# Attention with eight matmuls of values per unit or sixteen, and the entering batch's steps one to two units later

## The reference

```
h  = relu(layernorm(x))
z  = layernorm((L_norm @ h) @ Wc + bc) * g1 + be1
x1 = relu(z) + h
q, k, v = x1 @ Wq, x1 @ Wk, x1 @ Wv          # 4 heads
scores  = where(adjacency > 0, q k^T / sqrt(32), -1e9)
o  = softmax(scores) @ v                       # per head
x2 = layernorm(x1 + o @ Wo + bo) * g2 + be2
out = x + layernorm(x2 + gelu(x2 @ W1 + b1) @ W2 + b2) * g3 + be3
```

## Time and profile before

| | |
|---|---|
| median of 3 runs | 1015.18 us (1006.49 to 1015.77) |
| the profiled execution | 1019.77 us, its span 1017.9 us |
| mean granted clock of TensorE | 0.955 of 2.4 GHz |
| PE busy, share of the span | 937.3 us, 92% |
| DVE, ACT, POOL busy | 617.8, 535.1, 318.9 us (61%, 53%, 31%) |
| DMA moved | 61.54 MB; k and q take the greater part |

### The profile page before, as it was taken

One profiled execution on the slowest core, in us unless ns is written; L12 is line 12 of the kernel. 1 busy time (PEld: TensorE's weight loads), 2 busy tenths in 40 slices (PEclk: granted clock), 3 DMA queues, 4 the chain that ended last, 5 costly groups with the idle time before them and its releaser, 6 DMA issues. The chain is left out here.

```text
span 1017.9 us, 20046 instructions
## 1 busy us (share of the span) xinstructions
PE 937.3 (92%) x7078; PEld 757.7 (74%) x7078; DVE 617.8 (61%) x2003; ACT 535.1 (53%) x1176; POOL 318.9 (31%) x421
## 2 busy tenths in 40 slices
PE   5998999999999999989699999999999999876995
PEld 4556789999999999978466777777777777655774
DVE  3752333333333333524578988888888888864886
ACT  2232322222222233121588888888888888862674
POOL 0001101111111111203135544555555544222786
PEclk8887999999999999989799999999999999995998
DMA  3000000000000000003354444454545554500122
GB/s 91 1 1 10 11 1 12 20 10 10 10 10 10 10 10 10 12 1 102 87 131 116 118 114 116 114 121 110 124 125 125 126 125 126 126 2 1 42 62 63
DMA packets 47218, 61.54 MB, mean 60 GB/s; under 512 B 4377, under 2 KB 22050, under 8 KB 47138
## 3 DMA queue, kind: packets, MB, share of 16 engines
q1 hardware_dynamic: 47138, 60.51, 23.1%
HBM read 39.53 MB, written 20.97 MB: 59 GB/s over the span
## 5 line engine op out<-in xcount | busy, mean ns | idle before, releaser
L1562 ACT ACTIVATE prob<-prob,low 128x512 f32<-128x512 f32 x256 | 184.0, 719 | 51.4 <-DVE low L1614 49.5
L1614 DVE CUSTOM_DVE_ANT_0 prob<-bank,mask 128x512 f32<-128x512 f32 x256 | 171.5, 684 | 28.6 <-PE bank L1440 27.0
L1453 PE MATMUL bank<-ident,prob 128*128 128x128 f32 x1024 | 161.9, 281 | 12.0 <-ACT probT L1551 11.8
L1453 PEld LDWEIGHTS bank<-ident,prob 128*128 128x128 f32 x1024 | 113.8, 141 | 58.1 <-issue 31.7
L1440 PE MATMUL bank<-k_stack,q_stack 128*128 128x512 f32 x256 | 123.8, 485 | 10.2 <-DVE low L1614 5.0
L1551 ACT ACTIVATE probT<-bank 128x512 f32<-128x512 f32 x176 | 102.6, 583 | 2.9 <-PE bank L1453 1.1
L1083 DVE TENSOR_TENSOR T_lo<-bank,T_hi 128x512 fp32r<-128x512 f32 x48 | 33.1, 689 | 111.9 <-ACT T_hi L921 111.9
L921 ACT ACTIVATE T_hi<-bank 128x512 fp32r<-128x512 f32 x48 | 28.4, 592 | 134.7 <-PE bank L831 91.7
L619 POOL TENSOR_SCALAR var_eps<-mv 128x4 f32<-128x4 f32 x16 | 3.6, 226 | 297.7 <-DVE mv L1036 297.7
L927 ACT ACTIVATE Sq<-bank,trace_inv 128x512 fp32r<-128x512 f32 x64 | 44.0, 687 | 92.3 <-PE bank L754 92.3
L1473 PE MATMUL bank<-probT,v 128*32 128x128 f32 x2048 | 82.3, 279 | 3.2 <-ACT probT L1551 1.1
(11 more groups left out here) (241 smaller groups left out, 1948.1 us busy)
## 6 DMA issues: line engine op xcount, KB each, us to landing
k_stack<-bounce_q SPq DMA_DIRECT2D x64, 256.0 KB, 5.2
q_stack<-bounce_k SPq DMA_DIRECT2D x64, 256.0 KB, 7.6
bounce_q<-k_parts SPq DMA_DIRECT2D x16, 512.0 KB, 2.8
bounce_k<-q_parts SPq DMA_DIRECT2D x16, 512.0 KB, 3.1
x_in<-in_x_dram SPq DMA_DIRECT2D x16, 256.0 KB, 2.7
out_dram<-result SPq DMA_DIRECT2D x16, 256.0 KB, 2.2
A<-in_adj_dram SPq DMA_DIRECT2D x4, 256.0 KB, 3.3
W1s<-in_L_gnn_W_dram SPq DMA_DIRECT2D x1, 128.0 KB, 2.3
```

Of the source, the lines that this page charges most:

```text
L1453: last = pe.transpose(psum[2 + u % 2][:, mt * P:(mt + 1) * P], prob[u % RING][:, mt * P:(mt + 1) * P], ident[:, :])
L1562: act.activation(prob[u % RING][:, :], prob[u % RING][:, :], ACT.Exp, bias=low[:, u % TURNED:u % TURNED + 1], scale=-1.0, accum_out=row_su ...
L1614: dve.tensor_tensor_reduce(prob[u % RING][:, :], psum[u % 2][:, :], mask[:, u // HEADS, :], 1.0, 3e38, ALU.add, ALU.min, low[:, u % TURNED ...
```

## The change

The constants of the entering batch's steps and of the spread are raised by one or two units, and VALUES_STEP goes from 2 to 4. Nothing else is changed: the same instructions run, in another order on PE, ACT and DVE. By engine and unit:

- x1's transposes and x1T out from unit 2 to 3; the product with Wk and k_hi from 3 to 5; that with Wq and q_hi from 4 to 6; k_lo from 4 to 6, q_lo from 5 to 7
- the spread transposes from PE unit 3 to 4, their copy from ACT unit 4 to 5
- all four blocks of a tile's values in one unit: tile 0 in 7, tile 1 in 11, tile 2 in 15, tile 3 in unit 3 of the next round

SP's program is unchanged, and so is the unit of score 0, residual, v, oT, the convolution and the projection.

```
-AT_X1, AT_X1T, AT_X1T_OUT, AT_K, AT_Q, AT_K_HI, AT_Q_HI, AT_K_LO, AT_Q_LO = 1, 2, 2, 3, 4, 3, 4, 4, 5
+AT_X1, AT_X1T, AT_X1T_OUT, AT_K, AT_Q, AT_K_HI, AT_Q_HI, AT_K_LO, AT_Q_LO = 1, 3, 3, 5, 6, 5, 6, 6, 7
 AT_V, AT_V_OUT = 14, 14
 AT_CONV, AT_CONV_OUT, AT_Z, AT_Z_OUT, AT_Z_MOMENTS, AT_Z_STD = 6, 9, 10, 11, 12, 14
 AT_Y_MOMENTS, AT_H = 9, (11, 12, 13, 15)
-AT_RINV, AT_SPREAD, AT_SPREAD_OUT, AT_O, AT_PROJ, AT_Z2 = 0, 3, 4, 8, 11, 12
+AT_RINV, AT_SPREAD, AT_SPREAD_OUT, AT_O, AT_PROJ, AT_Z2 = 0, 4, 5, 8, 11, 12
 AT_Z2_MOMENTS, AT_Z2_STD = 3, 5
 TURN_LAG = 3
 VALUES_LAG = 7
-VALUES_STEP = 2
+VALUES_STEP = 4
```

## The result

The changed kernel takes 1055.2 us in the median of 4 runs (1048.2 to 1059.2); its ratio to the kernel before is 1.040 (95% interval 1.032 to 1.049), so 40 us slower where 26 were forecast. Put on the 1015.2 us of the kernel before, the ratio gives 1056.2, just over the upper end of the range, 1056. The profiled execution has a span of 1057.4 us, 39.5 more than before, at about the same mean granted clock (0.954). The attention from its first score matmul to its last takes 459.3 us against 416.0; the other stages, whose code is the same, take 4 less.

The account below looks back on a forecast made before the run. DVE and PE were taken to set the pace by turns, until moved steps make score 0 wait for q's loads. 23 us over 14 intervals plus 2.5 gave +25.5 on 1019.8, 1045; less 4.6 for the median, forecast 1041 us, range 1014 to 1056.

Parts of the forecast that it names:

- What bounds the kernel: Attention rounds of 26.37 us: PE looks like the bound, but DVE sets the pace in units 0 to 4, PE in 8 to 14.
- Rival (b): Attention: PE is the bound and its 0.9 us a round shows, 1002 us, if the landing takes under 10.7 us; chance 0.08.
- Values in one burst: Units 3, 7, 11, 15: saves 0.9 us of PE work a round; transposes 13 stand 0.44 us later, DVE waits.
- Later steps: Entering batch's steps one or two units later: the 0.5 us wait ahead of the spread transposes goes; ACT packed in units 4-6.
- About zero: Both edits on compute alone, per attention round: about zero, between bounds of -1.4 and +0.3 us.
- The ring over the loads: Score 0 to q write 14.8 us, then landing 13.15, then score 0, which waits: rounds of 28.0 us, 1.65 more.
- 14 x 1.65 = 23: Extra time over the 14 intervals between score 0 of batch 1 and of batch 15: 1.65 us each, +23 us.
- landing 13.15: Time from the q write to the landing of the last q load: 13.15 us in the mean, 12.3 to 13.6 read.
- 14.85: The ring's path from score 0 in unit 15 to the q write, in us, also given as 14.8.
- rival (c): Attention: more is lost than the wait, as the clock falls or landings stretch; +44 us, so 1059 us; chance 0.06.
- First round: First attention round already waits for the DMA, so the delay counts there: at most 3.3 us, taken as 2.5.
- Rival (a): Attention: the loads stay hidden, a round takes 26.5 us, first round +4, so 1020 us; chance 0.14.

Follow-up runs that it names:

- run 1: Kernel before with VALUES_STEP = 4 and no other edit: 1025.2 us, 1.0115 of the kernel before.
- run 7: Kernel before with VALUES_STEP = 4 and bursts one unit later, in units 8, 12, 0 and 4: 1014.1 us, 1.0003 of the kernel before.
- run 8: Changed kernel with three loads each of k and q, not four, and bursts one unit later: 1014.8 us, 1.0006 of the kernel before.
- run 11: Kernel before with products of k and q one unit later, three loads of each, bursts in units 8, 12, 0, 4: 1014.7 us, 1.0007 of before.
- run 6: Changed kernel with VALUES_STEP back at 2 and three loads each of k and q, not four: 1015.5 us, 1.0022 of the kernel before.
- run 10: Kernel before with products of k and q one unit later and three loads of each, not four: 1010.6 us, 0.9966 of the kernel before.
- run 3: Changed kernel with three loads each of k and q, not four (96 rows contracted, not 128): 1016.4 us, 1.0029 of the kernel before.
- run 2: Changed kernel with VALUES_STEP back at 2, so the later steps alone: 1044.1 us, 1.0307 of the kernel before.
- run 5: Kernel before with three loads each of k and q, not four (96 rows contracted): 1014.9 us, 1.0002 of the kernel before.
- run 9: Kernel before with products of k and q and their copies one unit later, not two: 1019.1 us, 1.0054 of the kernel before.
- run 4: Changed kernel with unit 12's four transposes done five times over ahead of score 0: 1051.2 us, 1.039 of the kernel before.

## Why the prediction was off, step by step

- **What bounds the kernel**: PE's busy time is not it, as forecast. In runs 1, 7, 8 and 11 less work on PE never made a kernel faster (against before, before, run 6 and run 10). Rival (b) is out for this stage: even where its condition was met, a landing of 10.5 us in the mean in run 8, the rounds took 26.49 and not 25.5. The Trainium skill, "Perfetto Trace Analysis", Identifying the Most-Contended Engine, says to work on the engine with the highest occupancy first, and warns against matmul busy time as that measure. Here the warning fits: PE is busy 25.16 us of a round of 26.37, and 0.9 us less of it gained nothing. That DVE's packed stretch takes PE's place is shown by run 1, where DVE waits for the burst; what holds the other orders at 26.4 us is not.
- **Values in one burst**: the price of its place was named and right in kind. I had it inside a bound of +0.3 us a round for compute alone; it is 0.63 a round by itself (run 1), and 0.2 for the whole change without the loads (run 3).
- **Later steps**: right. The wait ahead of the spread transposes went, as forecast, and its 0.5 us showed up nowhere (run 6). "About zero" for compute was right.
- **The ring over the loads**: right, and shown by runs 2, 3, 5 and 9. Score 0 to q write was forecast at 14.8 us; where the clock is full it is 14.6.
- **Its size, and here the sum failed.** The term "14 x 1.65 = 23" measured 13 x 2.79 + 3.3 = 39.6. Both parts of the ring are longer. First, "landing 13.15": q write to score 0 is 14.01 us, 0.86 more. Of this 0.35 goes with the six rounds in which k's write took 4.1 to 5.0 us; the other 0.5 is there in the rounds without a slow write too, and its cause is open. (In the kernel before, the slowest of the 14 later landings is 13.8 us, not 13.6; the mean holds.) Second, "14.85": 15.15 in the mean, 0.3 more, because the new wait lets the clock fall behind score 0, and the matmuls that the path starts with then take up to 1.8 times as long: 15.3 to 16.1 us in the rounds hit worst. Without the falls (run 4) the path is 14.58, so they cost 0.57 a round and the forecast path was 0.27 too long. I had both as rival (c), with 0.06; the clock at least is not a rival but a part of the forecast mechanism, since a wait of 1.6 us a round was forecast at the very place where the path starts. The last of the 14 rounds was also mis-sized: it was 24.8 us before, having no convolution of a next batch, and is set by the ring now (28.0).
- **First round**: forecast +2.5 us, measured +1.6 (27.7 to 29.3). From the last score 0 on it is +2.1 us, where I expected some tenths of gain; the clock was low there too, and in run 4, where it was not, it is +0.7.
- **Rival (a)** fell: in the changed kernel no round had 26.5 us, and the shortest write-to-score time was 13.0.

Open: why k's write is so much slower in the rounds in which code is loaded beside it, and whether that is the cause; the two go together over 195 rounds, and I did not try a kernel whose code is loaded at other times. Open too: what keeps the round at 26.4 us in four different orders (that of before and run 5, and those of runs 6, 7 and 11), while run 10 has 26.17.

## What to carry to other kernels

A step that feeds a transfer has a due time; before it is moved later, read for each round how far ahead of its first use the last transfer lands, and compare this slack with the move, including the slowest landings. Beyond the slack the cost is no longer the overrun alone, as transfer and first use close a ring, and every delay anywhere on it is paid in full in each round. If a move puts a new wait on TensorE, look at what runs right behind it: it may run at half the clock.

## What the runs showed of the hardware

- The granted clock fell to its lower level for 3.4 us behind single PE waits of 1.8 to 3.1 us (eight times in the changed kernel, four in run 2, once in run 3), in a stage where PE is otherwise busy about 90% of the time. It did not after all waits of that length, and behind no score 0 of batches 1 to 15 in run 4, where 1.7 us of repeated transposes stood in the place of the wait. Once each in the traces of runs 1, 5, 7 and 11 it fell in the last round with no such wait, behind several pauses of 0.2 to 0.9 us.
- A 0.5 MB write from SBUF to DRAM, that of k, lands 2.7 to 3.9 us after its issue in 164 of 195 rounds, and in 4.0 to 5.1 us in all 27 in which a 16 KB packet of the instruction queue starts 0.7 to 2.0 us behind the issue. That the packet is the cause is not shown.
- Contracting 96 rows in place of 128 leaves the time of the score matmul unchanged (0.48 us).
